# Sandwich of a state-space layer, experts and differential attention: the attention's opening laid beside the last experts' opening, and the pieces between state steps laid elsewhere in the step

## The reference

```python
# 1: state-space layer, 256 inner channels, 16 states
u, z = split(x @ W_in.T)
uc = silu(conv3(u) + conv_b)                 # depthwise, 3 taps along the tokens
B, C, dt = split(uc @ W_xproj.T)             # 16, 16, 8 columns
delta = softplus(dt @ W_dt.T + b_dt)
h = exp(delta * A) * h + (delta * uc) * B    # token by token, for each of 16 states
y = sum_n(h_n * C_n) + uc * D
out = (y * silu(z)) @ W_out.T
# 2: eight routed experts, two per token, and one shared expert
h = gelu(x @ W1[e]); out = sum_e(combine[e] * (h @ W2[e])) + gelu(x @ sW1) @ sW2
# 3: differential attention, 8 heads of two score maps each
w = softmax(q1 @ k1.T) - lam * softmax(q2 @ k2.T)
lam = exp(sum(lq1 * lk1)) - exp(sum(lq2 * lk2)) + LAMBDA_INIT
out = (gamma * rmsnorm(w @ v) * (1 - LAMBDA_INIT)) @ Wout
# 4: gated attention experts and gated MLP experts (not touched but for one wait)
```

## Time and profile before

| | us |
|---|---|
| median of 3 runs (3073.69 to 3076.74) | 3073.71 |
| the profiled execution | 3073.01 |
| its span, first to last instruction | 3070.9 |
| DVE busy over the span | 2202.3 |
| PE busy over the span | 2391.0 |
| ACT busy | 1696.2 |
| POOL busy | 1448.7 |

### The profile page before, as it was taken

How to read it: one execution, slowest core, us unless ns; L and a number is a source line. 1 busy time by engine, 2 the same in 40 slices (tenths; PEclk the granted TensorE clock), 3 DMA queues, 4 the chain that set the end, 5 groups by cost and what they waited for, 6 DMA issues and landing times.

```text
span 3070.9 us, 42340 instructions
## 1 busy us (share of the span) xinstructions
PE 2391.0 (78%) x15570; PEld 1711.5 (56%) x15570; DVE 2202.3 (72%) x3693; ACT 1696.2 (55%) x2621; POOL 1448.7 (47%) x1343
## 2 busy tenths in 40 slices
PE   2333579388488794999999999999999478767987
PEld 0101256156256572777677777777777356745675
DVE  5999999989986314888788878887888543354334
ACT  5333476376474342878777877787777224222322
POOL 0434323433433102655866676667567541564156
PEclk7555699698798896999999999999999789887988
DMA  3000000000000001101000000000000100000000
GB/s 103 0 0 0 1 1 1 0 1 1 0 1 1 1 1 40 26 24 29 21 23 22 22 22 22 22 22 21 22 22 1 42 1 1 1 14 1 1 1 14
DMA packets 32031, 42.04 MB, mean 14 GB/s; under 512 B 8897, under 2 KB 18130, under 8 KB 31442
## 3 DMA queue, kind: packets, MB, share of 16 engines
q1 hardware_dynamic: 31826, 39.34, 4.7%
HBM read 12.05 MB, written 2.10 MB: 5 GB/s over the span
## 4 chain that ended last, share of the span: by engine, by line
PE 49%; DVE 24%; issue 12%; POOL 9%; ACT 5%; SPq 1%; DMA 0%; POOLq 0%; DVEq 0%; ACTq 0%
PE ps L1073 10%; PE ps L1051 6%; PE ps L1062 6%; PE ps L828 5%; DVE MA L1209 3%; DVE lnb L315 2%; DVE BIG L340 2%; PE ps L757 2%; PE ps L1842 2%; PE ps L1033 2%; PE ps L759 2%; PE ps L758 2%; DVE BIG L334 2%; PE ps L1784 1%; DVE ps L328 1%
## 5 line engine op out<-in xcount | busy, mean ns | idle before, releaser
L1209 DVE TENSOR_REDUCE MA<-ps 128x1 f32<-128x1024 f32 x512 | 623.3, 1221 | 191.4 <-PE ps L1051 178.6
L423 POOL TENSOR_TENSOR MA<-MA,BIG 128x1024 f32<-128x1024 f32 x128 | 309.3, 2438 | 590.4 <-DVE BIG L340 559.1
L1073 PE MATMUL ps<-MA,WB 128*64 128x128 f32 x4096 | 504.4, 277 | 0.0
L1073 PEld LDWEIGHTS ps<-MA,WB 128*64 128x64 f32 x4096 | 442.6, 137 | 88.9 <-issue 87.9
L1051 PE MATMUL ps<-BIG 96*128 96x512 f16 x1024 | 313.8, 388 | 13.6 <-ACT WB L1136 5.0
L1136 ACT ACTIVATE WB<-ps,MA 128x1024 f32<-128x1024 f32 x206 | 229.7, 1115 | 149.2 <-DVE MA L1209 149.2
L828 PEld LDWEIGHTS ps<-WB,HR 128*128 128x128 f32 x2304 | 285.5, 199 | 32.5 <-issue 16.9
L828 PE MATMUL ps<-WB,HR 128*128 128x128 f32 x2304 | 295.5, 285 | 9.0 <-DVE acc L696 9.0
L744 ACT ACTIVATE HR<-ps,b 128x512 f32<-128x512 f32 x288 | 191.2, 687 | 174.1 <-PE ps L759 173.3
L1143 ACT ACTIVATE MA<-ps 128x1024 f32<-128x1024 f32 x256 | 259.9, 1015 | 5.0 <-PE ps L1062 5.0
L1605 POOL TENSOR_TENSOR BIG<-MA,BIG 128x512 f32<-128x512 f32 x128 | 132.2, 1049 | 232.3 <-PE ps L1828 74.5
(11 more groups left out here) (306 smaller groups left out, 5262.3 us busy)
## 6 DMA issues: line engine op xcount, KB each, us to landing
BIG<-BIG SPq DMA_DIRECT2D x192, 64.0 KB, 2.0
BIG<-WB SPq DMA_DIRECT2D x192, 64.0 KB, 2.0
WB<-w_dram SPq DMA_DIRECT2D x1, 2304.0 KB, 14.6
X<-x_dram SPq DMA_DIRECT2D x4, 512.0 KB, 12.5
HR<-w_dram SPq DMA_DIRECT2D x1, 2048.0 KB, 9.3
out_dram<-X SPq DMA_DIRECT2D x4, 512.0 KB, 3.2
WB<-wqkv_dram SPq DMA_DIRECT2D x1, 1536.0 KB, 6.3
WB<-w_dram SPq DMA_DIRECT2D x2, 512.0 KB, 8.3
```

The costliest lines, as they stand in the source:

```text
L423: e.tensor_tensor(yy[:, c, :], yy[:, c, :], db[n % 2][c], ALU.add).then_inc(*p_my.up(b, n, c))
L1073: x = e.matmul(bank[6][64 * pp:64 * pp + 64, 0:128], V[(4 * b + g) % 2][:, k, 64 * pp:64 * pp + 64], DT[n % 2][:, 128 * k:128 * k + 128], ...
L1209: e.tensor_reduce(L_of(n)[:, c:c + 1], ps[s][:, :], AX, ALU.max, negate=True).then_inc(*v_amx.up(n, s))
```

## The change

It has five parts.

1. The planned times are other numbers, some of them per batch now, and the loop's own pieces have planned times that shift tb against the rest. What is woven between the steps stands elsewhere.
2. The first tap of the convolution with its bias is made by ACT (Identity with scale and bias) instead of DVE.
3. B and C are taken apart by four DVE instructions instead of six, written straight into the rows' tile.
4. Attention's opening (`OPENING`, ORDER up to the first scores) is woven beside the experts of batch 3 on every engine. The tiles that it writes don't overlap those that the experts use. The barrier ahead of attention is gone; single waits take its place. Three weight transfers are issued by SP during the last loop, behind waits for the end of y of batch 2 and the first tb of batch 3. The four transfers of the last layer's norm weights (lnp) leave the constants at the program's start and are issued behind those.
5. A way to have ACT and POOL make the combines is written in (`WEIGHTED`), for the batches in a list that is empty.

```diff
-N_PERIOD, M_PERIOD, M_FIRST = 14.0, 224.0, 56.0
+N_PERIOD, M_PERIOD, M_FIRST = 13.11, 209.76, 56.0
...
+WEIGHTED = []
...
+LOOP_AT = {"tb": -3.75, "scan1": 2.72, "scan0": 4.94, "th": 7.2, "add": 9.43, "da": 0.34, "rows0": 4.86,
+           "rows1": 12.09, "z": 20.8, "zK": 1.47, "za": -0.43}
+A_AT = {"norm0": 1.02, "norm1": 3, "norm2": 9.74, "turn": 10.4, "op": 15, "opK": 2.4, "ope": 1, "v": 31.5,
+        "vK": 0.09, "lam": 4.33}
...
-                e.wait_ge(*a_m.at("u", b, c, 1))
-                if c == b == 0:
-                    e.wait_ge(*p_const.at("pad"))
-                e.tensor_scalar(cv[c], u[:, c, 0:1024], cw[:, c, 0:1], cb[:, c:c + 1], ALU.mult, ALU.add).then_inc(
-                    *dve_own.up())
                 for k in (1, 2):
-                    e.wait_ge(*dve_own.now())
+                    if k == 1:
+                        e.wait_ge(*a_mtap.at(b, c))
+                    else:
+                        e.wait_ge(*dve_own.now())
                     i = e.scalar_tensor_tensor(out=cv[c], in0=u[:, c, k:k + 1024], scalar=cw[:, c, k:k + 1], in1=cv[c],
                                                op0=ALU.mult, op1=ALU.add)
                     i.then_inc(*(dve_own.up() if k == 1 else v_mconv.up(b, c)))
-            r, hi = projected[0:96, :], rows[b % 2]
+            r, hi = projected, rows[b % 2]
             yield in_at(b, "bc1")
             e.wait_ge(*a_m.at("wx", b, 1))
-            e.tensor_copy(bc[0], r).then_inc(*dve_own.up())
+            e.tensor_copy(hi, r[0:96, :]).then_inc(*dve_own.up())
             e.wait_ge(*dve_own.now())
-            e.tensor_tensor(r, r, bc[0], ALU.subtract).then_inc(*dve_own.up())
+            e.tensor_tensor(r[0:64, :], r[0:64, :], hi[0:64, :], ALU.subtract).then_inc(*dve_own.up())
             e.wait_ge(*dve_own.now())
             yield in_at(b, "bc2")
-            e.tensor_copy(bc[1], r).then_inc(*dve_own.up())
+            e.tensor_copy(hi[0:64, :], r[0:64, :]).then_inc(*dve_own.up())
             e.wait_ge(*dve_own.now())
-            e.tensor_tensor(hi, r, bc[1], ALU.subtract).then_inc(*dve_own.up())
-            e.wait_ge(*dve_own.now())
-            e.tensor_copy(hi[32:64, :], bc[1][32:64, :])
-            e.tensor_copy(hi[0:32, :], bc[0][0:32, :]).then_inc(*v_mbc.up(b))
+            e.tensor_tensor(hi[0:32, :], r[0:32, :], hi[0:32, :], ALU.subtract).then_inc(*v_mbc.up(b))
...
+            for c in range(2):
+                yield in_at(b, f"tap{c}")
+                for h in range(2):
+                    e.wait_ge(*a_m.at("u", b, c, h))
+                if c == b == 0:
+                    e.wait_ge(*p_const.at("pad"))
+                if c and b:
+                    e.wait_ge(*v_mdl.at(b - 1, 0))
+                e.activation(cv[c], up[b % 2][:, c, 0:1024], ACT.Identity, bias=small["convb"][:, c:c + 1],
+                             scale=small["convw"][:, c, 0:1]).then_inc(*a_mtap.up(b, c))
...
-        for i in range(4):
-            consts += [(lnp[:, i, :], d["lnp"][i:i + 1, :].partition_broadcast(128)),
-                       (lam[:, i, :], d["lam"][i:i + 1, :].partition_broadcast(128))]
+        consts += [(lam[:, i, :], d["lam"][i:i + 1, :].partition_broadcast(128)) for i in range(4)]
...
+        OPENING = ORDER[:ORDER.index(("scores", 0, 0))]
+        ORDER = ORDER[len(OPENING):]
+
+        def opening_at(p, late=0.0):
+
+            if p[0] in ("norm", "turn"):
+                t = A_AT[f"norm{p[2]}"] if p[0] == "norm" else A_AT["turn"] + 1.3 * p[2]
+            elif p[0] == "op":
+                t = A_AT["op"] + A_AT["opK"] * (4 * p[3] + p[4])
+            else:
+                t = A_AT["v"] + A_AT["vK"] * p[3]
+            return f_at(NB - 1, "stats", t + late)
...
-            ring, n, free = [bank[7]], 0, [None]
-            for p in ORDER:
+            ring, n = [bank[i] for i in (0, 1, 2, 3)], 0
+            free = [a_m.at("out", NB - 1, 1), v_mscan.at(NB - 1, 15, 1), v_mth.at(NB - 1, 15, 0), v_mth.at(NB - 1, 15, 0)]
+            for p in OPENING + ORDER:
+                if p == ORDER[0]:
+                    opened.extend(free)
+                    ring, n, free = [bank[7]], 0, [v_fcb.at(NB - 1, 17)]
                 if p[0] == "end":
                     ring = [bank[i] for i in (7, 0, 1, 2, 3)]
                     n, free = 0, free + [a_ex.at(N_UNITS - 1, s) for s in (0, 0, 1, 1)]
...
-        wqk, wv = WB[:, 0:1024], WB[:, 1024:1536]
-        wout = WB[:, 1536:2048].rearrange("p (c n) -> p c n", c=4)
+        wqk, wv = MA[:, 2048:3072], MA[:, 3072:3584]
+        wout = MA[:, 3584:4096].rearrange("p (c n) -> p c n", c=4)
         stack = [BIG[:, 4096 * i:4096 * i + 4096].bitcast(F16).rearrange("p (w h t) -> p w h t", w=2, h=4) for i in range(2)]
-        hl = [ap2(x) for x in (BIG[:, 8192:9216], WB[:, 4096:5120])]
-        V = [WB[:, 2048 + 1024 * i:3072 + 1024 * i].rearrange("p (j n) -> p j n", j=8) for i in range(2)]
-        P_ = ([WB[:, 6144 + 1024 * i:7168 + 1024 * i] for i in range(3)] + [MA[:, 1024 * i:1024 * i + 1024] for i in range(3)]
+        hl = [ap2(x) for x in (BIG[:, 8192:9216], MA[:, 8192:9216])]
+        V = [x.rearrange("p (j n) -> p j n", j=8) for x in (MA[:, 9216:10240], MA[:, 0:1024])]
+        P_ = ([WB[:, 6144 + 1024 * i:7168 + 1024 * i] for i in range(3)] + [WB[:, 1024 * i:1024 * i + 1024] for i in range(3)]
               + [SEL[:, 2048 * i:2048 * i + 2048].bitcast(F32) for i in range(2)] + [WB[:, 5120:6144], BC[:, 0:2048].bitcast(F32)])
         osl = [OS[:, 128 * i:128 * i + 128] for i in range(2)]
-        DT = [MA[:, 3072 + 1024 * i:4096 + 1024 * i] for i in range(2)]
-        O_ = [MA[:, 5120:9216].rearrange("p (i n) -> p i n", i=8), HR[:, :].rearrange("p (i n) -> p i n", i=8)]
-        oT = [MA[:, 9216 + 512 * i:9728 + 512 * i] for i in range(2)]
+        DT = [WB[:, 3072 + 1024 * i:4096 + 1024 * i] for i in range(2)]
+        O_ = [MA[:, 4096:8192].rearrange("p (i n) -> p i n", i=8), HR[:, :].rearrange("p (i n) -> p i n", i=8)]
+        oT = [MA[:, 1024 + 512 * i:1536 + 512 * i] for i in range(2)]
         sq = [MA[:, 10240 + 512 * i:10752 + 512 * i] for i in range(2)]
...
+            for c in range(2):
+                e.wait_ge(*a_myy.at(NB - 1, c))
+            e.wait_ge(*v_mtb.at(NB - 1, 0, 1))
             e.dma_start(wqk, d["wqk"]).then_inc(s_wa, 16)
             e.dma_start(wv, d["wv"]).then_inc(s_wa, 16)
-            e.dma_start(WB[:, 1536:2048], d["wout"].rearrange("p c n -> p (c n)")).then_inc(s_wa, 16)
-            for p in ORDER:
+            e.dma_start(MA[:, 3584:4096], d["wout"].rearrange("p c n -> p (c n)")).then_inc(s_wa, 16)
+            if WEIGHTED:
+                e.wait_ge(*p_fcb.at(WEIGHTED[-1], 17))
+            for i in range(4):
+                e.dma_start(lnp[:, i, :], d["lnp"][i:i + 1, :].partition_broadcast(128)).then_inc(s_lnp, 16)
+            for p in OPENING + ORDER:
...
-                    elif q == 0:
-                        e.wait_ge(*v_lam.at(1))
+                    else:
+                        for c in range(2):
+                            e.wait_ge(*(p_my.at(NB - 1, 15, c) if q else v_mscan.at(NB - 1, 15, c)))
...
+                        for free in opened[2 * s:2 * s + 2]:
+                            e.wait_ge(*free)
...
+                    if n == s == 0:
+                        e.wait_ge(*t_fdn.at(NB - 1, 17))
...
+        def opening_act(e):
+            yield f_at(NB - 1, "stats", A_AT["lam"])
+            e.wait_ge(*v_lam.at(1))
+            e.activation(lsc[:, 2:4], lsc[:, 0:2], ACT.Exp, bias=0.0, scale=1.0).then_inc(*a_lam.up(0))
+            for p in OPENING:
+                yield opening_at(p, A_AT["ope"])
+                attend_act(e, [p])
...
+        def opening_dve(e):
+            yield f_at(NB - 1, "stats", A_AT["lam"])
+            e.tensor_tensor(lsq[:, 0:32], lam[:, 0, :], lam[:, 1, :], ALU.mult)
+            e.tensor_tensor(lsq[:, 32:64], lam[:, 2, :], lam[:, 3, :], ALU.mult).then_inc(*dve_own.up())
+            e.wait_ge(*dve_own.now())
+            e.tensor_reduce(lsc[:, 0:1], lsq[:, 0:32], AX, ALU.add).then_inc(*v_lam.up(0))
+            e.tensor_reduce(lsc[:, 1:2], lsq[:, 32:64], AX, ALU.add).then_inc(*v_lam.up(1))
+            e.wait_ge(*a_lam.at(0))
+            e.tensor_tensor(lsc[:, 4:5], lsc[:, 3:4], lsc[:, 2:3], ALU.subtract).then_inc(*dve_own.up())
+            e.wait_ge(*dve_own.now())
+            e.tensor_scalar(lsc[:, 5:6], lsc[:, 4:5], -LAMBDA_INIT, None, ALU.add).then_inc(*v_lam.up(2))
+            e.wait_ge(s_wa, 48)
+            e.tensor_scalar(wout, wout, small["gam"][:, 0:1], 1.0 - LAMBDA_INIT, ALU.mult, ALU.mult).then_inc(*v_lam.up(3))
+            for p in OPENING:
+                yield opening_at(p, 0 if p[0] == "norm" else A_AT["ope"] + 0.1)
+                attend_dve(e, [p])
...
+                e.wait_ge(s_lnp, 64)
...
             const_dve(e)
-            weave(weights_dve(e), over(loop_dve, e), over(front_dve, e), over(back_dve, e), over(moe_dve, e))
```

(9 more changed lines are left out.)

190 lines of the change are left out of this document (110 added, 80 removed).

## The result

The changed kernel takes 2962.24 us in the median of 4 runs (2951.87 to 2971.7), against 3073.7 before: a ratio of 0.9637, 95% interval [0.9596, 0.9678], 111 us less. 2930 was forecast, with 2895 to 2985 around it and 2910 to 2950 as the likeliest. The profiled execution is the slowest of the four, 2971.7 us with a span of 2969.5, 101.3 less than the 3073.0 of before; the steps are compared against it, so they come out some 10 us smaller in sum than between the medians.

A forecast was written before the change was run, and what follows sets the result against it. DVE was taken to bound loops 0 to 2, no longer alone in loop 3, and PE the last experts and attention. 3073.0 -101 (loops) -10 (behind loop 3) -31 (opening) -2 (lnp) = 2929, plus 0.7, 2930 us; range 2895 to 2985.

The forecast's parts named there:

- rival (c): Whole kernel: half of the excess of DVE's pieces stays, since static order isn't time; 2970 us, chance 0.14.
- the pieces beside POOL's adds: State loops: DVE's pieces, moved between the scans and th where POOL is idle, lose their excess duration, 81 us.
- The taps behind tb: Loop fronts: convolution taps right behind tb still meet POOL's second add; 3 us put back for three fronts.
- DVE's waits in the loops: The four loops' 78.4 us of DVE waits shrink by 12, 10 of it in loop 3; bounds 0 and 45.
- rival (a): Loops paced by the experts: DVE's gain in loops 1 and 2 becomes waits for down projections; 3004 us, chance 0.08.
- The first tap on ACT: Loops: moving the first convolution tap takes 8.6 us from DVE; ACT has room, late taps cost at most 6.
- Behind loop 3: From loop 3's end to the last experts' input statistics: 10 us less, between 3 and 14.
- The opening: Attention's start: first maximum 43 us earlier, price 12 at the last experts' start (bounds 5 and 18), net -31.
- PE's term: Price of the opening on PE at the last experts' start: 9 us, between 5 and 11.
- lnp: Program start: four norm weight transfers leave it, so 2 us less, none if x arrives last.
- Rival (d): Attention: probabilities and differences in other tiles make each difference slower, 1.65 instead of 0.88 us; 3127 us, chance 0.04.
- Rival (e): The change doesn't do what it says: true for the combines, counted at 0; for the whole, chance 0.02.

## Why the prediction was right, and where it wasn't

*The number.* 2962 lies in the range, but 32 above 2930 and outside the 2910 to 2950 that I called likeliest. The range reached up to it for rival (c), half of the excess staying (2970), and that isn't what happened: the excess went, and waits took its place. So the parts below were right in loop 0, behind loop 3 in size, and at the opening; that the time still fell into the range owes something to luck.

*The kernel's bound and the pieces beside POOL's adds.* DVE's excess was read rightly: 84 us of busy time went (89 forecast), the thinned adds show POOL's adds as the cause with no instruction moved, and one number of the table brings more than all of it back (111). Most of the 5 that are missing are a misreading: for the norm (L315) I took the mean duration, 0.73 and 0.64, less 0.27, but 0.27 is the busy time for each of eight instructions that overlap; their mean duration is 0.34. By busy time its three slowed groups gave 23 us (15.9, 13.6 and 10.6 became 6.4, 6.3 and 4.2), not the 27 that such a sum has. The taps behind tb were put at 3, or 3.7 if each pair waited for the rest of the add: two of the three did, for 1.16 each, 2.3 in all.

*DVE's waits in the loops: the term that failed.* The prediction let them fall from 78 to 66; they rose to 106, which is 40 of the 45 us that the loops missed. The step was "between 0 (the waits stay since PE's work is the same and DVE comes sooner) and 45": it had no end on the side where waits grow. What stood in its place was rival (a) in three fifths of its size (45 of the 74 us by which it lies above the forecast): with DVE's steps shorter, ACT's turns between two tables and PE's wait for them are what loops 1 and 2 go by; in loop 3, where the forecast had a gain of 10 and 1.6 came, PE's own work counts too. The row against (a), PE busy for 170 of 243 us, was the wrong row: PE was not full but waited in turn. The rows that would have told are PE's waits for ACT (L757 for L744, 14.7 us in loop 1 of before) and ACT's table loads. Without the loads DVE's idle time in the four loops is 63.4, and loops 1 to 3 come out near the forecast lengths, 215, 222 and 211.

*The first tap on ACT.* Its move was counted as 8.6 us of DVE's time won and nothing lost, at most 6. DVE's busy time did fall by 5.5 (761.6 to 756.1 in the loops), and the kernel still got longer by it: about 8 in the profiles at equal clock (1.6 at the start, 4 in loop 1, 2 in loop 2), some 10 by the ratios, and 16 to 19 between medians from different chips. "ACT is busy 139.5 of 243.4, so it has room" was the same mistake.

*Behind loop 3:* -9.8 for -10, right in size and not for the reason that I gave: the statistics and norm of batch 2's sum still stand ahead. One combine stands there, at 936.63, instead of three, and DVE's idle time fell from 14.9 to 7.3, since two waits for ACT (2.8 and 3.9) and one for the down projections (4.0) are gone.

*The opening:* -37.9 for -31. The gap lost 43.2, as forecast; the price was 5.3 (138.0 to 143.3) instead of 12. PE's term, taken at 9 between 5 and 11, was mis-sized: 3.8. Its work there is 9.1 us, since only the transposes and one pair of matmuls took as long as before and the rest half of it, so some 5 of it fell in rests that I had put at 3. DVE's small instructions cost 1.5, not 3: ACT answered in 0.27 instead of 1.61, since no table load of 1.28 stood ahead of its exponential.

*lnp:* ACT's first instruction came 1.6 earlier (2 forecast), and the tap took part of it back. *Rival (d)* fell: the differences have the same median of 877 ns. *Rival (e)*, for the combines, holds as counted: the list is empty and they stay on DVE. For the whole it fell.

## What to carry to other kernels

Two engines that hold each other up, as DVE and POOL do here in SBUF, can be kept apart by order alone: with the one's pieces where the other rests, neither took longer than alone (1.23 and 4.66 us). Before counting freed time of the busiest engine as won, take it away in the rows of the next chain: an engine that is busy 60% and waits in a ring with two others can already be a bound, and a wait of the freed engine will grow there. An estimate of waits needs an end on the side where they grow.

## What the runs showed of the hardware that was not expected

Beside POOL's pair of adds not only instructions with two SBUF inputs take longer (1.23 to 3.25 us): the norm, with one, does too (0.34 to 0.80), while tb, with one input in PSUM, stays at 1.21 (201.91, under the adds that start at 200.94).

ACT's table loads (1.283 us each, some 26 per loop between the exponential and the gelu) cost 8 to 17 us in each of two loops, although ACT is busy for only 62% of them.

The same program gets different granted clocks in one place: 16 us of loop 1 ran at 0.50 in one execution and at 0.89 in another, and the loop took 230.3 and 224.9 us. With fewer matmuls the mean clock of loop 1 fell to 0.75, and the loop took 229.8.
